# Four engine queues of a fused attention and feed-forward kernel, each block with an order of its own

## What is computed

```python
h = _layernorm(x) * (1 + ca) + sa
x = x + ga * attn(h)              # 16 heads of 64
h = _layernorm(x) * (1 + cb) + sb
x = x + gb * ffn(h)

# attn, per batch
q, k, v = h @ Wq, h @ Wkv[:, :1024], h @ Wkv[:, 1024:]        # split in heads
s = (q * scale) @ k.T
gm = max(s, axis=-1)              # over the whole row, before the mask
p = where(causal_mask, 0.0, exp(s - gm))
out = (p @ v) / (sum(p) + 1e-8)
return out @ Wo + bo

# ffn, per batch; both operands of each linear layer go through a blockwise 4-bit quantization
gate, y = fp4_linear(h, w_gate), fp4_linear(h, w_up)
return fp4_linear(silu(gate) * y, w_down)
```

## Time and profile before

| | us |
|---|---|
| median of 3 runs | 1324.75 (1322.56 to 1326.55) |
| the profiled execution | 1323.2 |
| its span, first to last instruction | 1321.3 |
| PE busy | 1270.0 (96%) |
| weight loads on PE | 1033.1 (78%) |
| DVE busy | 1089.7 (82%) |
| POOL busy | 841.2 (64%) |
| ACT busy | 837.1 (63%) |

### The profile page before, as it was taken

How to read it: one execution, slowest core, us unless ns; L and a number is a source line. 1 busy time by engine, 2 the same in 40 slices (tenths; PEclk the granted TensorE clock), 3 DMA queues, 4 the chain that set the end, 5 groups by cost and what they waited for, 6 DMA issues and landing times.

```text
span 1321.3 us, 34181 instructions
## 1 busy us (share of the span) xinstructions
PE 1270.0 (96%) x10194; PEld 1033.1 (78%) x10194; DVE 1089.7 (82%) x2565; ACT 837.1 (63%) x2885; POOL 841.2 (64%) x1582
## 2 busy tenths in 40 slices
PE   4999999999999999999999999999999999999984
PEld 3678888788888788888788888888888878888863
DVE  5678888888888888888888888888888888888775
ACT  3666657667667666666766666766666766666640
POOL 1656666766666766666666666676666676666664
PEclk9999999999999999999999999999999999999995
DMA  3000000000000000000000000000000000000000
GB/s 103 18 19 18 12 22 18 22 22 16 12 20 18 22 22 16 20 12 20 20 22 20 17 10 22 18 22 22 16 11 21 18 22 22 16 22 6 19 19 10
DMA packets 38056, 26.53 MB, mean 20 GB/s; under 512 B 2800, under 2 KB 33392, under 8 KB 38032
## 3 DMA queue, kind: packets, MB, share of 16 engines
q1 hardware_dynamic: 38032, 26.23, 7.0%
HBM read 21.94 MB, written 4.28 MB: 20 GB/s over the span
## 4 chain that ended last, share of the span: by engine, by line
PE 92%; DVE 4%; ACT 2%; issue 1%; DMA 1%; POOL 1%; SPq 0%; DVEq 0%; POOLq 0%; ACTq 0%
PE ps_m L827 27%; PE ps_s L922 18%; PE ps_m L806 16%; PE ps_o L949 14%; PE ps_m L873 9%; PE ps_s L931 5%; PE ps_m L897 4%; ACT probs L563 1%; DMA wkv<-L_attn_Wkv 1%; DVE neg_max L736 1%; DVE probs_t L662 0%; DVE qy L62 0%; ACT qk L531 0%; DVE amax L54 0%; DVE qm L66 0%
## 5 line engine op out<-in xcount | busy, mean ns | idle before, releaser
L563 ACT ACTIVATE probs<-ps_s,neg_max 128x128 f32<-128x128 f32 (+1 forms) x1024 | 424.4, 429 | 396.0 <-PE ps_s L931 396.0
L437 POOL TENSOR_SCALAR probs<-probs,r_den 128x256 f32<-128x256 f32 (+1 forms) x768 | 347.6, 468 | 0.0
L736 DVE TENSOR_REDUCE neg_max<-ps_s 128x4 f32<-128x1024 f32 x256 | 303.9, 1218 | 2.5 <-PE ps_s L922 2.3
L922 PE MATMUL ps_s<-qk 64*128 64x256 f32 x2048 | 259.1, 392 | 0.8 <-ACT qk L531 0.8
L662 DVE COPY probs_t<-ps_m 128x512 f32<-128x512 f32 x256 | 176.4, 689 | 80.2 <-PE ps_m L806 76.2
L806 PE MATMUL ps_m<-ident,probs 128*128 128x128 f32 x1536 | 230.9, 273 | 2.4 <-POOL probs L437 1.0
L435 POOL TENSOR_TENSOR probs<-probs,r_den 128x128 f32<-128x128 f32 x256 | 102.1, 399 | 202.5 <-DVE r_den L745 183.8
L922 PEld LDWEIGHTS ps_s<-qk 64*128 64x128 f32 x2048 | 185.3, 187 | 48.3 <-issue 12.3
L563 ACT ACTIVATION_READ_ACCUMULATOR probs<-ps_s,neg_max 128x1 f32 x1024 | 217.7, 213 | 0.0
L73 POOL TENSOR_TENSOR qy<-qy,qm 128x352 f32<-128x352 f32 (+1 forms) x96 | 82.9, 864 | 181.7 <-DVE qm L66 179.4
L949 PE MATMUL ps_o<-probs_t,v 128*64 128x256 f32 (+1 forms) x2048 | 194.7, 332 | 1.5 <-ACT o_t L555 1.5
(11 more groups left out here) (107 smaller groups left out, 1794.2 us busy)
## 6 DMA issues: line engine op xcount, KB each, us to landing
mod_a<-mod_rows SPq DMA_DIRECT2D x32, 256.0 KB, 3.3
x_in<-L_attn_x SPq DMA_DIRECT2D x32, 128.0 KB, 2.1
x_res<-L_attn_x SPq DMA_DIRECT2D x32, 128.0 KB, 2.1
out<-y_out SPq DMA_DIRECT2D x32, 128.0 KB, 1.8
mod_b<-mod_rows SPq DMA_DIRECT2D x32, 64.0 KB, 2.9
wkv<-L_attn_Wkv SPq DMA_DIRECT2D x2, 512.0 KB, 6.9
wq<-L_attn_Wq SPq DMA_DIRECT2D x1, 512.0 KB, 4.1
wo<-L_attn_Wo SPq DMA_DIRECT2D x1, 512.0 KB, 8.2
```

What stands on the lines that cost most here:

```text
L437: ins = nc.gpsimd.tensor_scalar(cols, cols, r_den[:, u % 4, s:s + 1], 1.0, ALU.mult, ALU.mult)
L563: ins = nc.scalar.activation(probs[:, u % 4, h, t * P:(1 + 2 * t) * P], ps_s[:, 2 * (u % 2) + h, t * N:t * N + (1 + t) * P], ACT.Exp, bias ...
L736: nc.vector.tensor_reduce(neg_max[:, u % 4, :], ps_s[:, 2 * (u % 2):2 * (u % 2) + 2, :].rearrange("p b (t j) -> p (b t) j", t=2), AX.X, AL ...
L922: mm = nc.tensor.matmul(ps_s[:, 2 * (u % 2) + h, t * N:(t + 1) * N], qk[rows, u % 4, 0, t * P:(t + 1) * P], qk[rows, u % 4, 1, :], start=( ...
```

## The change

Each block gets an order of its own, written out, on PE, DVE, ACT and POOL. Both DVE and ACT can now read any of the transposes and copy the attention outputs: whichever of them lists the step does it. ACT takes t0, t1 and t2 of block 1, t1 of blocks 2 and 3, and the output copies of blocks 1 and 3; DVE takes the other seven t copies and the output copies of blocks 0 and 2. The kinds, shapes and numbers of all other instructions stay, SP's queue stays, and so do the semaphores. The code that does the work becomes small functions with the conditions inside (`input_stats`, `attended_normalized`, `ffn_in_scales`, `keep`, `modulate` and so on); their bodies are the old ones and are left out here.

```diff
         SHARED = (
-            ("t0", "qk0", "t1", ("v", 0, 0), ("xqt", 2, 0), "qk1", "t2", ("gate", 2, 0), ("v", 0, 1)),
-            ("t0", "qk0", "t1", ("up", 2, 0), ("gate", 2, 1), "t2", "qk1", ("up", 2, 1), ("wo", 1, 0), ("wo", 1, 1)),
-            ("t0", "qk0", "t1", ("v", 0, 2), ("hqt", 2, 0), "t2", "qk1", ("v", 0, 3), ("xt", -1, 0)),
-            ("t0", "qk0", "t1", ("down", 2, 0), "t2", ("hqt", 2, 1), "qk1", ("down", 2, 1)))
+            (("v", 0, 0), ("xqt", 2, 0), "qk0", "qk1", "t0", ("v", 0, 1), "t1", "t2", ("gate", 2, 0), ("up", 2, 0), ("gate", 2, 1)),
+            ("t0", "qk0", "t1", ("wo", 1, 0), ("up", 2, 1), "t2", "qk1", ("wo", 1, 1)),
+            ("t0", "t1", ("v", 0, 2), "t2", ("v", 0, 3), "qk0", "qk1", ("hqt", 2, 0), ("xt", -1, 0)),
+            (("hqt", 2, 1), "t0", ("down", 2, 0), "t1", "qk0", "t2", ("down", 2, 1), "qk1"))
...
-        WEIGHT_PLACES = [(0, 7), (1, 3), (1, 4)]
+        WEIGHT_PLACES = [(0, 8), (0, 9), (0, 10)]
...
-        T_ON_ACT = (2,)
```

POOL (the weights' rounding of iteration 0 goes to the head of blocks 1 to 3):

```diff
+                for j in range(PAIRS):
+                    if i_is(i, 0) and j > 0:
+                        pool.wait_ge(setup_dve, SETUP_MAGIC)
+                        quantize_round(nc.gpsimd, Steps(pool, weights_round, done=j - 1), wfq, WB // BLOCK, scale_w,
+                                       qy_w, qm_w, parts=(j - 1,))
+                    if j == 0:
+                        normalize(i, -1)
+                        normalize(i, 0)
+                    elif j == 1:
+                        keep()
+                        normalize(i, 1)
+                        input_rstd()
+                        residual()
+                        round_hidden(i - 2, 0)
+                        normalize(i, 2)
+                        attended_rstd()
+                    elif j == 2:
+                        normalize(i, 3)
+                        normalize(i, 4)
+                    elif j == 3:
+                        modulate()
+                        round_hidden(i - 2, 1)
+                        normalize(i, 5)
+                        round_ffn_in()
+                        normalize(i, 6)
```

ACT:

```diff
-                        if kind == "t" and k % 3 in T_ON_ACT:
+                        if kind == "t":
...
+                    if j == 0:
+                        exponentials(0, 0)
+                        shared_reads(0)
+                        shared_reads(2)
+                        shared_reads(3)
+                        shared_reads(5)
+                        exponentials(0, 1)
+                        exponentials(1, 0)
+                        shared_reads(8)
+                        exponentials(1, 1)
+                        shared_reads(10)
+                    elif j == 1:
+                        shared_reads(0)
+                        out_copy()
+                        shared_reads(1)
+                        exponentials(2, 0)
+                        exponentials(2, 1)
+                        shared_reads(2)
+                        shared_reads(5)
+                        exponentials(3, 0)
+                        exponentials(3, 1)
+                        shared_reads(6)
+                    elif j == 2:
+                        exponentials(4, 0)
+                        exponentials(4, 1)
+                        shared_reads(1)
+                        shared_reads(2)
+                        exponentials(5, 0)
+                        shared_reads(4)
+                        shared_reads(5)
+                        shared_reads(6)
+                        exponentials(5, 1)
+                        shared_reads(8)
+                        shared_reads(7)
+                    elif j == 3:
+                        exponentials(6, 0)
+                        shared_reads(0)
+                        out_copy()
+                        exponentials(6, 1)
+                        shared_reads(3)
+                        shared_reads(4)
+                        exponentials(7, 0)
+                        exponentials(7, 1)
+                        shared_reads(7)
```

DVE:

```diff
-                    if kind == "t" and k % 3 not in T_ON_ACT:
+                    if kind == "t":
...
+                def out_copy():
+                    if has.unit(2 * (j - 2)):
+                        at = 2 * ((j - 2) % PAIRS)
+                        dve.wait_ge(o_full, PAIRS * i + j - 1)
+                        nc.vector.tensor_copy(o_t[:, at:at + 2, :], ps_o[:, :].rearrange("p (u j) -> p u j", u=2)).then_inc(ot_ready, 1)
...
+                    if j == 0:
+                        maxima(0)
+                        denominators(-1)
+                        out_copy()
+                        shared_reads(0, 1)
+                        maxima(1)
+                        shared_reads(0, 4)
+                        shared_reads(0, 6)
+                        shared_reads(0, 7)
+                        shared_reads(0, 8)
+                        denominators(0)
+                        shared_reads(0, 9)
+                        shared_reads(0, 10)
+                    elif j == 1:
+                        maxima(2)
+                        denominators(1)
+                        hidden_scales(i - 2, 0)
+                        input_stats()
+                        maxima(3)
+                        hidden_magic(i - 2, 0)
+                        shared_reads(1, 3)
+                        shared_reads(1, 4)
+                        hidden_scales(i - 2, 1)
+                        denominators(2)
+                        shared_reads(1, 7)
+                        attended_stats()
+                    elif j == 2:
+                        denominators(3)
+                        maxima(4)
+                        maxima(5)
+                        input_normalized()
+                        shared_reads(2, 0)
+                        out_copy()
+                        denominators(4)
+                        shared_reads(2, 3)
+                        attended_normalized()
+                    elif j == 3:
+                        hidden_magic(i - 2, 1)
+                        ffn_in_scales()
+                        maxima(6)
+                        denominators(5)
+                        maxima(7)
+                        shared_reads(3, 1)
+                        h_low_part()
+                        shared_reads(3, 2)
+                        shared_reads(3, 6)
+                        shared_reads(3, 5)
+                        denominators(6)
+                        ffn_in_magic()
```

PE, where `scores` of both units and `values` still open each block, and then:

```diff
+                    if j == 0:
+                        mask(0, 0)
+                        mask(0, 1)
+                        at_place(0, 0)
+                        at_place(0, 1)
+                        at_place(0, 2)
+                        at_place(0, 3)
+                        at_place(0, 4)
+                        at_place(0, 5)
+                        at_place(0, 6)
+                        at_place(0, 7)
+                        mask(1, 0)
+                        mask(1, 1)
+                        at_place(0, 8)
+                        at_place(0, 9)
+                        at_place(0, 10)
+                    elif j == 1:
+                        at_place(1, 0)
+                        at_place(1, 1)
+                        at_place(1, 2)
+                        mask(2, 0)
+                        mask(2, 1)
+                        at_place(1, 3)
+                        mask(3, 0)
+                        at_place(1, 4)
+                        mask(3, 1)
+                        at_place(1, 5)
+                        at_place(1, 6)
+                        at_place(1, 7)
+                    elif j == 2:
+                        mask(4, 0)
+                        at_place(2, 0)
+                        mask(4, 1)
+                        at_place(2, 1)
+                        at_place(2, 2)
+                        mask(5, 0)
+                        mask(5, 1)
+                        at_place(2, 3)
+                        at_place(2, 4)
+                        at_place(2, 5)
+                        at_place(2, 6)
+                        at_place(2, 7)
+                        at_place(2, 8)
+                    elif j == 3:
+                        mask(6, 0)
+                        at_place(3, 0)
+                        mask(6, 1)
+                        at_place(3, 1)
+                        at_place(3, 2)
+                        at_place(3, 3)
+                        mask(7, 0)
+                        mask(7, 1)
+                        at_place(3, 4)
+                        at_place(3, 5)
+                        at_place(3, 6)
+                        at_place(3, 7)
```

More of the change, by code:

```diff
@@ L552, in out_copy @@
                     def out_copy():
+                        if not has.unit(2 * (j - 2)):
+                            return
                         at = 2 * ((j - 2) % PAIRS)
@@ L557, in exponentials @@
                     def exponentials(u, h):
+                        if not has.attn:
+                            return
```

(12 more changed lines are left out.)

125 lines of the change are left out of this document (46 added, 79 removed).

## The result

The changed kernel takes 1358.01 us (median of 4 runs, 1357.31 to 1359.62) against 1323.75 for the kernel before beside it: ratio 1.0258, 95% interval 1.0244 to 1.0272, **slower by 34 us** where I had forecast 4 to 5 us less. The profiled span is 1356.2 us against 1321.3. The granted TensorE clock is 0.982 of full speed against 0.988, but that is not what makes the 34 us: the other three runs of the changed kernel had 0.986 and took as long, and in batches 3 to 30 it is 1.00 in both traces.

The account below looks back on a forecast made before the run. PE (TensorE) was taken to bound the kernel, with 1.6 us of waits per batch to win from. Middle -13, start +2 and end +6 gave -5 us on the median 1324.75: 1320, range 1304 to 1334.

Parts of the forecast that it names:

- DVE sets the pace: Rival: VectorE's work orders the batch; net -23 us, with the ends 1310; chance 0.1.
- The middle: Steady-state batches: period shortens from 39.24 to 38.8 us, a gain of 0.44 x 29 batches = 13 us.
- other bank reads: One of the small waits per batch, for reads of banks outside the three loops: 0.1 us.
- 37.7 for PE's work without a wait: Sum of PE's matmul groups per batch, priced from profile rows as if nothing waited: 37.7 us.
- 1.6 of waits a batch: PE's waits of 0.1 to 0.3 us each per batch, 4%; removing them could win at most 48 us.
- Loop A: Block seam: from down 1's end through ffn_in_magic to xqt, 5.5 us against 5.05 of PE; lost 0.45.
- Loop B: Block 2 to 3: from t2 through POOL's modulation and rounding to hqt 1, 6.7 us against 6.2; lost 0.5.
- hqt 1 in block 3 waiting 0.3 for POOL's hq: Sign of being right: PE's hidden-activation transposes in block 3 wait 0.3 us for POOL's rounding.
- Loop C: Block 1 to 2, after the second output projection: 5.55 us against 5.4 of PE; lost 0.15, upper bound 1.6.
- The start: First batches: late denominators(0) and weights make block 2 about 4 us late, 1.5 to 2 given back; +2 (0 to 5).
- The end: Drain: the preparation waits for down 1's read, 4.2 us, and wo is late by 1 to 2; +6 (3 to 8).
- slower: the seam: Rival: the block-seam loop loses more than 0.9 us, so 1333 to 1337, deciding from period 38.97; chance 0.25.

Follow-up runs that it names:

- s4_outcopy: Changed kernel with the attention-output copies of blocks 0 and 2 given back to ScalarE, first in its blocks; 1357.18 us, ratio 1.0243.
- s1_stats: Changed kernel with the next input's statistics moved on VectorE from block 1 to block 0, behind the copy of t2; 1341.22 us, ratio 1.0123.
- s10_pool: s7_four with block 3's GpSimd hidden rounding and normalize(5) ahead of modulation (except in the drain), VectorE's ffn_in_scales behind reads of t0 and down 0; 1321.69 us, 0.9977.
- s2_seam: Changed kernel with ffn_in_magic moved on VectorE from the end of block 3 to ahead of the read of down 1; 1351.16 us, ratio 1.0192.
- s5_three: Changed kernel with the VectorE moves of s1_stats, s2_seam and s3_weights together; 1332.75 us, ratio 1.0052.
- s6: s1_stats with maxima(6) ahead of ffn_in_scales in VectorE's block 3; 1341.66 us, ratio 1.0122.
- s7_four: s5_three with maxima(6) ahead of ffn_in_scales in VectorE's block 3; 1331.08 us, ratio 1.0047.
- s3_weights: Changed kernel with VectorE's one-time weights' preparation in iteration 0 moved ahead of denominators(0); 1356.76 us, ratio 1.0238.
- s12_weights: s11_start with POOL's three weight-rounding steps in iteration 0 moved behind normalize(1), normalize(3) and normalize(5); 1322.04 us, ratio 0.9969.
- s11_start: s10_pool with, in iteration 0, unit 1's masks ahead of place 1 and exponentials of units 0 and 1 between the first projection copies; 1320.91 us, 0.9974.

## Why the prediction was wrong

**The frame held.** PE's instructions were unchanged, waits for other engines' places in the queue made the difference, and VectorE's total was no bound (s4_outcopy against s1_stats). The rival "DVE sets the pace" falls with that. The Trainium skill's Perfetto Trace Analysis (Identifying the Most-Contended Engine) would name VectorE here by occupancy, 82% against 78% of weight loads; in this case that share did not say where the time was.

**The middle, -13 predicted, +21.7 measured.** Two terms of my sum failed, one that I put at almost nothing and one that I priced too low.

The first: I wrote that VectorE "has 18% of the span idle, so only its place counts", and then put "other bank reads" into the small ones: 0.1. **That step failed: block 1 alone was 0.63.** It gives VectorE two maxima, two sets of hidden scales, one preparation, two sets of statistics and the reads of wo 0, up 1 and wo 1, and its queue runs from 631.9 to the end of the block with one gap of 0.23; every read of a `ps_m` bank that stands in it is late. s1_stats moves 0.7 us out and gets 0.63 back. I looked for loops at the block seams only.

The second: **37.7 for PE's work without a wait was too low**, and so the 1.6 of waits a batch, and the 48 us that could be won, were too high. In s10_pool PE has no idle time at all in batches 3 to 30 (busy 1088.3 of 1088.3 us), and the batch takes 38.87; the kernel before had 4.7 us idle there. By distances between starts in that trace, the twelve groups of transposes take 5.0 a batch, where I had 12 x 0.36 = 4.3; gate and up take 2.2 instead of 2.0, and the other terms are within 0.1 of mine. Matmul ends are modelled, so whether part of this is short waits stays open.

The period of 40.03 against 38.8 is 1.23 off: +0.63 for block 1, -0.42 since A and B cost 0.53 together and not 0.95, and +1.0 for the second term (38.87 with all three undone, where my sum says 37.7 + 1.35 - 0.25 - 0.45 - 0.5, about 37.9). Either failed term alone, added to 38.8, puts the period over 39.

**Loop A**, 0.45: s2_seam gives 0.12 with block 1 as it was, and 0.18 is the difference of s5_three and s1_stats. So it was there, and smaller. **Loop B**, 0.5: s10_pool shortens the batch by 0.35 (39.22 to 38.87), and s6, s7 and s10 together show that it is held by POOL's modulation, as I had it; but "hqt 1 in block 3 waiting 0.3 for POOL's hq" was covered in the kernel after by a wait that I hadn't priced, VectorE's `ffn_in_scales`, which stands ahead of `maxima(6)` and waits for POOL (25.6 us over 31 times): the mask waited first. **Loop C**: the x_in normalization took 0.84 a pair (at 646.95) and not 2.0, so 0.61 was the nearer end; of the loop's 0.15 no run says anything. The kernel before with nothing but the moved copies was not run.

**The start, +2 predicted, +7.2 measured.** That "block 2 starts about 4 us late" was right: 22.8 after the first score (44.04 less 21.23) against 18.4. "The next, short batch gives back 1.5 to 2" was wrong: blocks 2 and 3 lost another 1.6, part of it at the lower clock, batches 1 and 2 another 0.7, and the first score came 0.5 late. Of the causes that I named, the weights' preparation behind the late `denominators(0)` and POOL's rounding ahead of `normalize(1)` are each worth over 2 us in batch 0 (s3_weights 2.3, s12_weights 2.2); with the first undone, moving exponentials(0,1) ahead of the copies (s11_start) gave nothing that can be told from the spread.

**The end, +6 predicted, +6.1 measured**, and the 4.2 for the preparation behind down 1 was 4.3 in s2_seam. The other 1 to 2, for a late wo, was not tried, so that the sum fits so well may be luck.

**The rival "slower: the seam"** had the sign, and the period was over its 38.97; but its mechanism fell, since undoing the seam gave 0.12 to 0.18 a batch, and its price was 1333 to 1337. Of the signs that I listed as wrong, one showed, a period over 39. First masks waited too, but less than the 0.4 that I had named: 0.17 at the seam (3.70 after the block's scores, 3.54 in s2_seam) and 0.37 in block 3 (3.90, and 3.53 in s7_four).

## What to carry to other kernels

When engines run written-out orders, the share of busy time says nothing about a block: add up what each queue must do **between two reads that free a buffer**, and look for the block which that sum fills (0.7 us moved out of a full one gave 0.63 a batch, 1.36 us of copies moved off the same engine elsewhere 0.07). When a wait is removed and nothing moves, look for the producer under both waits; here the gain came from putting POOL's urgent rounding ahead of a modulation that could be patient. A price for "no wait" that is put together from the shortest rows is a guess until a trace without idle time shows it. When steps that share rotating banks are exchanged, write down again which pairs now share one. And walk the unrolled first iterations separately, since an order that suits the steady state can put one-time work ahead of the chain that starts the pipeline.

## What the runs showed of the hardware

A tiny VectorE operation can take as long as a large one of GpSimd. In the kernel after, at the start (VectorE's timeline):

```profile
35.19 2.07 DVE L807 TENSOR_SCALAR den_eps<-den 128x4 f32<-128x4 f32 x1
37.30 0.18 DVE L810 RECIPROCAL r_den<-den_eps 128x4 f32<-128x4 f32 x1
```

Four elements per partition took 2.07 us where the median of 256 is 0.16. It ends at 37.26, and POOL's weights' step, begun at 34.67, ends at 37.24; the reciprocal behind it took the 0.18 that it takes everywhere. In block 1 above, `qm` took 0.76 at 638.15, beside POOL's x_gb (637.60 to 638.70), where the one behind it took 0.34; `scale` took 0.18 at 635.17 and 0.75 at 641.46, beside a rounding step of POOL (641.39 to 642.18). The 0.18 ran beside POOL too, beside a one-input multiplication (from 635.14). Max reductions and the operations on PSUM kept their times. The Trainium skill has this (SBUF — State Buffer, section SBUF: two separate sides): an operation of two SBUF inputs, or one in a mode that uses both ports, takes the pair that GpSimd also uses as an exclusive lock for the whole instruction. I had weighed it only for the normalization with two inputs; the traces agree for one-input float32 operations beside POOL's two-input ones, and in a full block these stretches are part of what fills it. They do not agree beside POOL's one-input multiplications. In the kernel after, of the `scale` and `den_eps` operations begun in the middle of a POOL operation, those beside a two-input one never ended ahead of it (0 of 128), and those beside a one-input one all did (57 of 57, about 0.27 ahead of its end), at their usual time. In the kernel before, 31 `den_eps` beside POOL's two-input `rstd` of 128x2 kept their 0.16 too, so the number of inputs is not the whole rule. The share of these stretches in the 0.63 was not tried by itself.
